# A decoder layer on one core: other order of the context keys, distance corrections on two squares, slopes in the keys' rows, no reset of rows, all six tiles summed by GpSimd

## The reference

```python
x = x + self_attention(layernorm(x))           # 16 heads of 32, with biases
x = x + cross_attention(layernorm(x), context) # 16 heads of 32, 224 queries, 750 keys
x = x + mixture_of_experts(x)  # 8 experts, best 2, hidden 1024
```

```python
rel = jnp.abs(jnp.arange(Nk)[None, :] - jnp.arange(Nq)[:, None] - (Nk - Nq))
bias = -slopes[:, None, None] * rel.astype(jnp.float32)
scores = jnp.einsum('bhqd,bhkd->bhqk', q, k) * scale + bias[None]
```

## Time and profile before

| what | value |
|---|---|
| median of 3 runs | 1865.44 us (1862.95 to 1866.67) |
| profiled execution: its time, its span | 1864.92 us, 1863.2 us |
| mean granted clock of PE, share of full | 0.973 |
| PE, weight loads, DVE, ACT, POOL busy | 93%, 74%, 57%, 40%, 41% of the span |
| cross phase, first to last instruction of it | about 722.8 to 1230 us |
| plain iteration 16, from its first `second_scores` to the next one's | 971.54 to 983.52 us |

### The profile page before, as it was taken

One profiled execution on the slowest core, in us unless ns is written; L12 is line 12 of the kernel. 1 busy time (PEld: TensorE's weight loads), 2 busy tenths in 40 slices (PEclk: granted clock), 3 DMA queues, 4 the chain that ended last, 5 costly groups with the idle time before them and its releaser, 6 DMA issues. The chain is left out here.

```text
span 1863.2 us, 34969 instructions
## 1 busy us (share of the span) xinstructions
PE 1732.1 (93%) x11164; PEld 1383.3 (74%) x11164; DVE 1064.2 (57%) x1897; ACT 753.5 (40%) x1364; POOL 757.2 (41%) x848
## 2 busy tenths in 40 slices
PE   6987999999999897999999999879999999999997
PEld 6776778777777676777777777657787787887775
DVE  5553455565555545776777877584554545445553
ACT  3333333433333333654555545522442424224441
POOL 3100223323323322777777757532542425124541
PEclk9998899999999997999999999979999999999999
DMA  7635665665665846996877667243764646446773
GB/s 227 211 129 171 166 172 172 180 171 167 176 180 156 209 126 134 185 194 141 179 152 152 142 137 182 90 127 90 246 218 115 220 113 220 113 122 213 226 238 90
DMA packets 212066, 309.81 MB, mean 166 GB/s; under 512 B 21984, under 2 KB 151712, under 8 KB 207440
## 3 DMA queue, kind: packets, MB, share of 16 engines
q1 hardware_dynamic: 186640, 223.96, 45.1%
q0 software_dynamic: 15808, 41.10, 10.2%
q10 hardware_dynamic: 9504, 43.26, 6.4%
HBM read 224.62 MB, written 83.62 MB: 165 GB/s over the span
## 5 line engine op out<-in xcount | busy, mean ns | idle before, releaser
L1937 DVE TENSOR_REDUCE a_part_max<-a_s_bank 112x1 f32<-112x500 f32 (+1 forms) x384 | 236.8, 673 | 82.9 <-PE a_s_bank L1682 64.4
L1843 ACT ACTIVATE a_prob<-a_st_bank 125x448 f32<-125x448 f32 x384 | 193.3, 545 | 108.7 <-PE a_st_bank L1700 70.2
L2556 DVE TENSOR_TENSOR e_u_sb<-e_u_bank,e_b_row 128x512 f32<-128x512 f32 x134 | 92.2, 688 | 224.5 <-PE e_u_bank L2321 218.0
L2319 PE MATMUL e_u_bank<-e_w_hi,e_xT_hi 128*128 128x512 f32 x536 | 213.9, 399 | 1.2 <-DVE e_w_lo L2549 0.4
L2321 PE MATMUL e_u_bank<-e_w_hi,e_xT_lo 128*128 128x512 f32 x536 | 210.6, 393 | 0.0
L2320 PE MATMUL e_u_bank<-e_w_lo,e_xT_hi 128*128 128x512 f32 x536 | 210.0, 392 | 0.0
L2479 POOL DMA_INDIRECT out<-l_rows,e_y_row x33 | 53.0, 1605 | 314.9 <-ACT l_rows L2433 161.3
L1543 POOL TENSOR_TENSOR a_part_sum<-a_prob 125x448 f32<-125x448 f32 x128 | 147.2, 1152 | 82.7 <-ACT a_prob L1843 82.3
L2380 ACT ACTIVATE e_g_hi<-e_g_bank 128x256 fp32r<-128x256 f32 x133 | 51.1, 384 | 311.9 <-PE e_g_bank L2328 286.5
L849 POOL TENSOR_TENSOR m_prob_sum<-m_prob 112x224 f32<-112x224 f32 x128 | 85.2, 671 | 170.9 <-ACT m_prob L1057 170.4
L2319 PEld LDWEIGHTS e_u_bank<-e_w_hi,e_xT_hi 128*128 128x128 f32 x536 | 101.3, 189 | 25.1 <-DVE e_xT_lo L2544 3.9
(11 more groups left out here) (380 smaller groups left out, 4486.2 us busy)
## 6 DMA issues: line engine op xcount, KB each, us to landing
e_w_raw<-L_ffn_Wl SPq DMA_DIRECT2D x96, 512.0 KB, 8.6
e_b_row<-L_ffn_bl ACTq DMA_DIRECT2D x33, 1024.0 KB, 5.8
k<-m_kt_hi SPq DMA_DIRECT2D x48, 250.0 KB, 3.2
k<-m_kt_lo SPq DMA_DIRECT2D x48, 250.0 KB, 4.2
m_c_in<-ctx POOLq DMA_DIRECT2D x12, 896.0 KB, 10.1
m_q_st<-q SPq DMA_DIRECT2D x96, 112.0 KB, 3.1
m_k_st<-k SPq DMA_DIRECT2D x96, 112.0 KB, 3.1
v<-m_cv SPq DMA_DIRECT2D x48, 224.0 KB
```

The lines of the kernel that those rows point to most:

```text
L1843: act.activation(prob[s % 2][:, hh, 2 * u:2 * u + 2, :], st_bank[n % SB][0:CR, 0:2 * S].rearrange("p (e q) -> p e q", e=2), ACT.Exp).then_ ...
L1937: dve.tensor_reduce(out, scores, AX.X, ALU.max).then_inc(s_free, 1)
L2319: pe.matmul(out, xT_hi[:, slot, k, :], w_h, start=(k == 0), stop=False)
L2556: dve.tensor_tensor(u_sb[:, q % 2, :, :], u_bank[q % 2][:, :].rearrange("p (h n) -> p h n", h=2), b1_row[:, slot, :, HC * q:HC * q + HC], ...
```

## The change

- The host reorders each batch's context rows by `KEY_RUNS`: keys 0 to 499, then 638 to 749, then 500 to 637, so that in the last two tiles of 125 keys the linear rows (now with a sign for each key) give the penalty exactly, save in two squares of 112 x 112 in which the sign changes inside. There a correction of twice the positive part (Relu in place of Abs) is added. So `rel_q` and `rel_k` have 224 columns in place of 500 and 448, and so have the matmuls with `d_hi` and `d_lo`.
- The slopes move from the query rows to the key rows. The 16 small sets of query rows (two ACT and one DVE instruction and one transfer each) go from the opening; DVE gets twelve instructions on key rows of up to 64 x 750 in the third chunk, POOL builds other constants. Row loads of a group are three transfers in place of two.
- `row_max` is 112 x 8 for a query tile: four constant columns and four maxima. `turn_max` transposes all eight, and ACT (`query_rows`) writes all eight rows afresh each step, at once. POOL's `reset`, and PE's wait for it, are gone. PE's first scores use only the upper rows (KD, 100 rows in place of 104).
- For s < 25 POOL adds tiles 4, 5 for all four heads (eight additions), and PE sums two tiles for each head; from 25 on the sums are as before.

```diff
+KEY_RUNS = [(0, CTX - 2 * CR, 0, 1), (CTX - 2 * CR, QR, SHIFT + QR, -1),
+            (CTX - 2 * CR + QR, CR - QR, CTX - 2 * CR, 1), (CTX - CR, CR, SHIFT + QR - CR, 1)]
...
-                    if head_beside(n, ch, m) is not None:
-                        query_slopes(head_beside(n, ch, m))
...
-                    act.activation(q_lin[:, :], grid[:, :], ACT.Copy, scale=slope(hd))
-                    act.activation(q_lin_hi[:, :], grid[:, :], ACT.Copy, scale=slope(hd)).then_inc(qlin_ready, 1)
...
-                        dve.scalar_tensor_tensor(q_rows[:, hd % 2, :], as_f32(q_lin_hi[:, :]), is_lo[:, :], q_lin[:, :], ALU.mult, ALU.add).then_inc(qrows_ready, 1)
...
+                        row_then(dve.tensor_scalar(k_lin[:, :], k_lin[:, :], no_key[:, :], slopes[:, :], ALU.mult, ALU.mult))
+                    elif part == 2:
+                        row_then(dve.tensor_scalar(grid[:, :], grid[:, :], has_key[:, :], slopes[:, :], ALU.mult, ALU.mult))
+                    elif part == 3:
+                        row_then(dve.tensor_tensor(k_lin[:, :], k_lin[:, :], grid[:, :], ALU.add))
+                    else:
+                        row_then(dve.tensor_copy(k_rows, k_lin[:, :]))
+                        row_then(dve.scalar_tensor_tensor(k_rows, grid[:, :], is_lo[:, :], k_lin[:, :], ALU.mult, ALU.add))
...
-        rel_q = c.sb("a_rel_q", [QR, 2, FAR], F32R)
-        rel_k = c.sb("a_rel_k", [CR, 2, S], F32R)
+
+        rel_q = c.sb("a_rel_q", [QR, 2, QR], F32R)
+        rel_k = c.sb("a_rel_k", [CR, 2, QR], F32R)
...
-        row_max = c.sb("a_row_max", [QR, 2, 4])
+
+        row_max = c.sb("a_row_max", [QR, 2, 8])
...
-                    sp.dma_start(as_f32(k_st[i][KQ:KB, :, :]), k_rows).then_inc(rows_loaded[i], DMA)
-                    sp.dma_start(as_f32(q_st[i][KQ:KB, :, :]), q_rows[:, i, :, :]).then_inc(rows_loaded[i], DMA)
+                    sp.dma_start(as_f32(k_st[i][KQ:KD, :, :]), k_lin[i].rearrange("h r c -> r h c")).then_inc(rows_loaded[i], DMA)
+                    sp.dma_start(as_f32(k_st[i][KD:KB, :, :]), k_hot).then_inc(rows_loaded[i], DMA)
+                    sp.dma_start(as_f32(q_st[i][KQ:KD, :, :]), q_rows).then_inc(rows_loaded[i], DMA)
...
-                        if hh < whole_heads(s):
+                        if s < STORING:
...
-                    pool.memset(as_f32(q_st[s % SLOTS][KQ:KQ + 4, :, :]), 0.0).then_inc(reset_done, 1)
-                    pool.wait_ge(reset_done, s + 1)
...
-                        if s >= SLOTS:
-                            pe.wait_ge(reset_done, s - SLOTS + 1)
...
-                        last = pe.matmul(bank[0:QR, 0:2 * FAR], d_hi[0:QR, hd, 0:QR], rel_q[:, :, :].rearrange("p t n -> p (t n)"),
+
+                        last = pe.matmul(bank[0:QR, FAR - QR:FAR + QR], d_hi[0:QR, hd, 0:QR], rel_q[:, :, :].rearrange("p t n -> p (t n)"),
...
-                        out, r = bank[0:CR, 0:2 * S], rel_k[:, :, :]
+                        out, r = bank[0:CR, QR:QR + S], rel_k[:, :, :].rearrange("p t n -> p (t n)")
...
-                        last = pe.transpose(bank[0:4, QR * t:QR * t + QR], row_max[:, t, :], ident[0:QR, 0:QR])
+                        last = pe.transpose(bank[0:8, QR * t:QR * t + QR], row_max[:, t, :], ident[0:QR, 0:QR])
...
-                    for n, (weights, t) in enumerate([(prob, 4), (prob, 5), (part_sum, 0), (part_sum, 1)]):
-                        for hh in range(whole_heads(s) if n < 2 else 0, 4):
+                    tiles = [(part_sum, 0), (part_sum, 1)] if s < STORING else [(prob, 4), (prob, 5), (part_sum, 0), (part_sum, 1)]
+                    for weights, t in tiles:
+                        for hh in range(4):
...
-                    act.activation(q_st[s % SLOTS][KQ:KQ + 4, :, :], st_bank[n % SB][0:4, 0:S].unsqueeze(1).broadcast_to([4, 4, S]),
+                    act.activation(q_st[s % SLOTS][KQ:KB, :, :], st_bank[n % SB][0:8, 0:S].unsqueeze(1).broadcast_to([8, 4, S]),
...
-                    dve.tensor_reduce(row_max[:, :, :].rearrange("p t h -> p h t"), part_max[:, :, :, :], AX.X, ALU.max).then_inc(max_ready, 1)
+                    dve.tensor_reduce(row_max[:, :, 4:8].rearrange("p t h -> p h t"), part_max[:, :, :, :], AX.X, ALU.max).then_inc(max_ready, 1)
...
+    order = np.concatenate([np.arange(key, key + n) for _, n, key, _ in KEY_RUNS])
+    arrays["ctx_1024"] = np.ascontiguousarray(arrays["ctx_1024"][:, order, :])
```

More of the change, by code:

```diff
@@ new lines, in _ @@
+                then(pool.iota(number[:, :], pattern=[[0, 1]], base=0, channel_multiplier=1))
+                then(pool.memset(slopes[:, :], slope(HEADS - 1)))
+                for hd in reversed(range(HEADS - 1)):
+                    then(pool.affine_select(out=slopes[:, :], in_=slopes[:, :], compare_op=ALU.is_ge, fill=slope(hd), base=-4 * (hd + 1),
+                                            pattern=[[0, 1]], channel_multiplier=1))
+                pool.sem_inc(grid_ready, 1)
+                then(pool.iota(q_rows[:, :], pattern=[[1, S]], base=0, channel_multiplier=0, allow_small_or_imprecise_dtypes=True))
@@ L1222, in _, with cross_phase @@
                 queries_lo(B - 1)
-def cross_phase(nc, sems, *, q, k, v, x1, k_rows, q_rows, first, second, third, w_out, b_out, w_route, b_route, choice_bias, x2, h_out, own_rows, first_h, routing, places, experts, signals, w1, w2, ident):
+def cross_phase(nc, sems, *, q, k, v, x1, k_lin, k_hot, q_rows, first, second, third, w_out, b_out, w_route, b_route, choice_bias, x2, h_out, own_rows, first_h, routing, places, experts, signals, w1, w2, ident):
     NK, RP = CTX // CR, 3
@@ L1413, in batch_at @@
             return (s - 4 - phase) // 4 if s >= 4 + phase and s % 4 == phase else None
-        def whole_heads(s):
-            return 3 if s < STORING else 0
         def sums_before(s):
-            return sum(4 + whole_heads(n) for n in range(s))
+            return 4 * s + 4 * min(s, STORING)
         with nc.Block() as block:
@@ L1612, in _ @@
                 sums(0)
-                reset(0)
                 for s in range(STEPS):
@@ L1866, in _ @@
                 act.wait_ge(rel_ready, 1)
-                act.activation(rel_q[:, :, :], rel_qf[:, :, :], ACT.Abs).then_inc(abs_ready, 1)
-                act.activation(rel_k[:, :, :], rel_kf[:, :, :], ACT.Abs).then_inc(abs_ready, 1)
+                act.activation(rel_q[:, :, :], rel_qf[:, :, :], ACT.Relu).then_inc(rest_ready, 1)
+                act.activation(rel_k[:, :, :], rel_kf[:, :, :], ACT.Relu).then_inc(rest_ready, 1)
                 diagonals(1)
                 diagonals(2)
-                minus_max(0)
+                query_rows(0)
                 for s in range(-1, STEPS):
```

145 lines of the change are left out of this document (77 added, 68 removed).

## The result

| kernel | median | runs | ratio to before, 95% interval |
|---|---|---|---|
| before, same chip | 1866.06 us | 1859.74 to 1870.57 (6) | |
| after | 1851.87 us | 1849.85 to 1856.41 (6) | 0.993 [0.9907, 0.9954] |

A forecast was written before the change was run, and what follows sets the result against it. PE was taken to bound the kernel, busy 93% of the span. Savings of 34.2 + 14.2 = 48.4 us less 8.5 of losses left 40, so 1825 us; the range of 8 in 10 was 1812 to 1840.

The forecast's parts named there:

- parts 1 and 2: Cross phase on PE: narrower corrections save 1.07 us a step, 34.2 in all; POOL's extra sums save 0.57 in 25 iterations, 14.2.
- Part 3: Whether DVE, ACT, POOL and transfers keep up: 0.16 us of new waits, a plain iteration of 10.5 us, no transfer wait.
- Iteration 5, where I feared POOL: First output projection waits for POOL's split of step 4, after six plain iterations: 1.5 us lost.
- early transfers: Loads in the first six iterations might hold them to their present pace, costing 7 us; no wait was taken.
- iterations 12 and 20, that begin with DVE late from the choice of experts: Loss term for these two cross-phase iterations: half a microsecond each, 1.0 us together.
- the one for iteration 3: Loss term: DVE splits a weight ahead of its maxima, so most of part 1 is not won, 0.8 us.
- rival 1: Another engine takes over the pace through DVE, POOL or early transfers: gain 10 to 28 us, 1837 to 1855; chance 0.10.
- a POOL-paced iteration: POOL's 10.8 us might set a plain iteration in place of 10.5, costing 3 us in all.
- Rival 3: PE, less packed, falls to 1.2 GHz; a loss from seven half-clock iterations on, 1891 us with ten; chance 0.04.
- not won: In square-root iterations two of four heads lie behind ACT: 0.33 of the 1.07 us lost, 2.0 for six.
- The small waits at each iteration's end: New PE waits, 0.25 us at each iteration's end, named as what could lower the clock.
- The opening: Part 4, before the cross phase: removed ACT, DVE and POOL work brings 0 us, with -3 and +3 as ends.

The follow-up runs named there:

- e1: The changed kernel with head 3's last two tiles summed by PE again, so seven POOL additions; 0.9942 of before, 1853 us.
- e3: The changed kernel with rel_q and rel_k padded with zeros to their former 500 and 448 columns; 1.0009 of before, 1866 us.
- e2: The kernel before with only the fourth head's tiles 4 and 5 added by POOL, the eighth addition; 1.0022 of before, 1869 us.
- e5: The changed kernel with POOL's additions held until DVE's chain is done in iterations 3, 12, 20, 21, 25, 28 and 29; 0.9874 of before, second chip.
- e6: e2 with the same waits on POOL as in e5; 0.9976 of before, second chip.
- e4: The changed kernel with unread matmuls in PE's waits: eight in square-root iterations, twelve in iterations 12 and 20; 0.9878 of before.
- e7: e5 with eight unread matmuls ahead of the third head in the iterations with a square root; 0.9847 of before, second chip.
- e10b: e7 run again unchanged, on a third chip; 0.9846 of before.

## Why the prediction was wrong

The ideal of iterations -1 to 29, by parts 1 and 2, is 25 x 1.64 + 6 x 1.07 = 47.4 us (iteration -1 has no sums, and from 25 on they are as before); 11.6 were won there. The 35.9 that are missing, by iteration (after's length less before's, plus 1.64 or 1.07; one execution of each, and the places where the clock falls differ from one execution to the next):

| where | predicted loss | measured loss |
|---|---|---|
| 12 and 20 | 1.0 | 11.0 |
| 21, 25, 29 | part of 1.0 | 8.0 |
| square roots (6 to 26) | 2.0 | 6.7 |
| 3 | 0.8 | 4.5 |
| -1 and 0 | 0.8 with the start-up | 3.8 |
| 27, 28 | part of 1.0 | -0.6 |
| plain and the rest, 5 included | 1.4 and 1.5 | 2.5 |

The opening and the start-up brought 4.0 us together, and the stretch from iteration 30 on gave back 1.5. So 4.0 + 11.6 - 1.5 = 14.1, the difference of the spans. The 1.5 is no more than the spread of that stretch on this chip (676.7 to 678.8 us).

- **What bounds the kernel, parts 1 and 2.** Right in a plain iteration, each to 0.06 us. The width brought 0.93 (11.98 in before, 11.05 in e1) to 0.97 (e3), and 1.07 less the 0.16 of waits for DVE is 0.91. The sums, with ACT's rows behind them, brought 0.56 (e1) to 0.57 (e2), where 0.57 was said.
- **Part 3, plain iterations, POOL and transfers.** Right. Iteration 5, where I feared POOL, lost 0.3. Iterations 1 and 2 took 10.56 and 10.82, so the early transfers held nobody.
- **The failed step: the term of the sum for "iterations 12 and 20, that begin with DVE late from the choice of experts, half a microsecond each by my estimate", and the one for iteration 3.** Put at 1.0 and 0.8 us together, they measured 5.8, 5.2 and 4.5. In iteration 12, taking e5 as the reference: 1.7 us contention, 1.9 half clock, and 2.2 (12.65 against 10.5) that are left with POOL held, four times my estimate. Of these, 0.56 are `a_zb` beside POOL's last addition; the rest is DVE's lateness with the chain at its old length. I had the chain's 3 us in the trace and didn't put it against the slack of three banks as I had done for the plain iteration. Other chains of DVE stand before iterations 21, 25 and 29; PE waited 1.41 and 1.61 us for the maxima in 21 and 25, and I gave these two no term. In 29 the longest wait, 1.04 us, has no releaser in the profile, so its 2.2 us are only in part DVE's. In iteration 3 the waits for DVE and ACT were 1.24 and 0.73 us, and 6.8 us of it ran at the half clock.
- **Why it was missed: rival 1.** The time fell in its interval, and another engine did hold PE, but not by what it priced: early transfers and a POOL-paced iteration did not come. "the extra additions run beside maxima from a bank, where they keep 1.15" is true of the maxima, and wrong as a dismissal: `choose`, `slots`, `a_w_lo` and `a_d_lo` have two inputs in SBUF. The row of before with POOL's 1.72 us showed that contention from the other side. Before, `choose` fell into a pause of POOL; eight additions in a shorter iteration close the pause.
- **Rival 3, the clock.** I gave it 0.04 and set it aside because 1.87 us of waiting had left the clock at 1.00 in one window. That wait has grown to 2.20, by the 0.33 that I myself had counted as "not won", and behind it the clock fell in iterations 6, 10 and 14, three of the six. The growth alone does not explain it: in e2, e3 and e6, where the wait is 1.87 as in before, the clock fell behind 3, 5 and 2 of the six. One window of one execution was too little to set the rival aside. The small waits at each iteration's end, which I named as its cause, did not do it: in after every plain iteration from 1 on ran at 2.4 GHz throughout. The Trainium skill, TensorE: Matmul & The Clock Gate, section "A second HAM failure mode: psum-queue depth-cycling", speaks of such small idle times; here they did nothing, and the clock fell behind single waits, of 1.0 to 3.3 us in after. It did not make the change a loss; after has 37 us of half clock more than before, about three iterations' worth (a stretch at that clock is some 13 us), not seven.
- **The opening.** 0 was taken, with 3 either way; the cross phase starts 3.5 us earlier, at 719.4. That is half a microsecond beyond the end, but the same opening brings e1, e3 and e4, on the same chip, to 717.1, 719.7 and 719.4. PE's longest wait on `p_hT_lo` is 1.39 to 2.34 us in after, e1, e3, e4 and e5, which lack the slopes' 16 sets of rows, and 4.0 to 4.3 in e2 and e6, which have them. Before, DVE stood 6.75 us for a store of v (`v<-p_v_sb`), after 2.61. Which of the instructions or transfers made that store late was not tried.

Open is why iteration 0 begins at half clock in every kernel with the narrow rows of the change (not in e2 and e6), what is left in 25, what shortened 27 to 29 in e5, and what makes the clock fall behind one wait and not behind an equal one.

## What to carry to other kernels

When work is given to GpSimd because it has room, look for the vector engine's instructions with two SBUF inputs that now run beside it: a tiny one can wait until GpSimd's instruction ends, and a chain of tiny ones in front of a critical release pays several times; a wait on GpSimd's side, which has room, mends most of it (iteration 12 from 16.31 to 12.65 us; about half a per cent of the kernel, measured across chips). When PE's work shrinks, list the chains of the other engines that don't shrink and weigh each against the banks' slack, not only in the plain iteration. A wait of PE can cost more than its length: its price is the wait plus, at times, the half clock behind it, so one window at full clock behind one such wait is no proof that it is free. Harmless matmuls in the wait can be cheaper.

## What the runs showed of the hardware

- A DVE instruction on 112 x 32 elements took 1.09 us in place of 0.19 and one on 112 x 8 up to about a microsecond, as long as GpSimd's addition had still to run; the end came 0.01 to 0.05 us behind GpSimd's. Which of the two waits is not told by the begins: in before and e5 an addition of 1.15 us took 1.72 and 1.57 beside two subtractions that kept their 0.48, in after the subtractions took 1.52 and the addition 1.19.
- The same wait does not always have the same effect on PE's clock. Behind the square roots it fell after 1, 3, 5 and 2 of 6 waits of 1.87 us (before, e2, e3, e6) and after 3, 4 and 4 of 6 of 2.20 us (after, e1, e5), and after both waits of 3.27 us (after). A wait of 1.53 us in iteration 12 left it at 2.4 GHz in e5; in e7 it fell there. In iteration 20, behind the same wait, it fell in e10b and not in e7, which are the same kernel.
- Eight unread matmuls of 500 columns in a wait of 2.20 us cost nothing that can be seen: the iteration takes 13.64 us with them, 13.62 without them at full clock.
